# Inverse roots of variances and squared norms as powers on GpSimd

## The reference, cut to what matters

```python
# in each of the 6 layers
qkv = x @ Wqkv                        # 16 heads of 64
q = l2norm(q) * qs                    # t / max(norm(t), 1e-12), per head and token
k = l2norm(k) * ksc
...                                   # rotary, softmax(q k^T * 8) in windows of 32, values
mu = x.mean(-1, keepdims=True)
var = ((x - mu) ** 2).mean(-1, keepdims=True)
xn = (x - mu) / jnp.sqrt(var + 1e-05) * g + bln
...                                   # a * gelu(gate) @ W2 + b2
```

## Time and profile before

| | us |
|---|---|
| Median of three runs | 3716.87 (3713.0 to 3719.67) |
| The profiled execution, its time | 3724.61 |
| Its span | 3722.6 |
| PE busy | 3402.5 (91%) |
| DVE busy | 3223.6 (87%) |
| ACT busy | 2227.8 (60%) |
| POOL busy | 2052.1 (55%) |

### The profile page before, as it was taken

The page is one execution under the profiler, slowest core; times in us unless marked ns, Lnnn a source line. Parts: engine busy times, 40 slices in busy tenths (PEclk is TensorE's granted clock), DMA queues, the critical chain, the costliest instruction groups (busy, mean ns, idle before and its releaser), DMA issues.

```text
span 3722.6 us, 144192 instructions
## 1 busy us (share of the span) xinstructions
PE 3402.5 (91%) x62248; PEld 1871.9 (50%) x62248; DVE 3223.6 (87%) x5344; ACT 2227.8 (60%) x3808; POOL 2052.1 (55%) x1787
## 2 busy tenths in 40 slices
PE   6899999999999999985676799999999999999996
PEld 2455555555555555542333355555555555555553
DVE  5899999999999999874776799999999999999984
ACT  3566576665666666652453466666766667666663
POOL 3666566555666656642433565665656656565552
PEclk8999999999999999996877999999999999999998
DMA  4232332232332322200001332232232332332320
GB/s 126 68 79 70 75 81 73 72 81 70 80 77 70 85 70 72 73 17 12 0 0 54 78 76 73 70 87 69 73 85 67 78 83 67 77 82 66 77 49 24
DMA packets 200483, 250.08 MB, mean 67 GB/s; under 512 B 52012, under 2 KB 95656, under 8 KB 199848
## 3 DMA queue, kind: packets, MB, share of 16 engines
q1 hardware_dynamic: 199848, 240.86, 25.9%
HBM read 36.18 MB, written 3.15 MB: 11 GB/s over the span
## 4 chain that ended last, share of the span: by engine, by line
PE 30%; DVE 12%; issue 4%; ACT 3%; POOL 1%; DMA 1%; SPq 0%; POOLq 0%; DVEq 0%; ACTq 0%
PE general L566 4%; PE attp L580 4%; PE general L628 3%; PE scores L598 3%; PE sums L608 2%; PE general L636 2%; PE general L645 2%; PE general L638 1%; PE proj_k L554 1%; DVE k_ring L1232 1%; DVE sines L752 1%; DVE q_ring L758 1%; DVE probs_t L845 1%; PE proj_q L554 1%; PE proj_q L556 1%
## 5 line engine op out<-in xcount | busy, mean ns | idle before, releaser
L1107 POOL TENSOR_TENSOR k_ring<-k_ring,partner 128x512 f32<-128x512 f32 x384 | 499.0, 1299 | 362.1 <-DMA partner<-sines 359.9
L1116 POOL TENSOR_TENSOR probs<-probs,q_scale 128x512 f32<-128x512 f32 x384 | 401.8, 1046 | 396.8 <-DVE probs L828 396.8
L1122 POOL TENSOR_TENSOR probs<-probs,row_sum 128x512 f32<-128x512 f32 x384 | 407.8, 1062 | 358.3 <-DVE row_sum L839 358.2
L1107 POOL TENSOR_TENSOR q_ring<-q_ring,partner 128x512 f32<-128x512 f32 x384 | 491.2, 1279 | 50.4 <-DMA partner<-sines 50.4
L954 ACT ACTIVATE squares<-proj_q 128x512 f32<-128x512 f32 x384 | 229.0, 596 | 402.4 <-PE proj_q L556 401.0
L580 PEld LDWEIGHTS attp<-probs_t,v_buf 32*64 32x64 f32 x24576 | 393.0, 133 | 147.4 <-issue 141.8
L566 PE MATMUL general<-att,wo 128*128 128x512 f32 x768 | 376.2, 624 | 74.0 <-ACT att L1013 74.0
L580 PE MATMUL attp<-probs_t,v_buf 32*64 32x64 f32 (+1 forms) x24576 | 435.5, 218 | 5.1 <-ACT att L1013 5.1
L752 DVE SCALAR_TENSOR_TENSOR sines<-proj_q,vec,consts 128x512 f32<-128x512 f32 x384 | 278.7, 726 | 170.1 <-ACT squares L954 149.7
L628 PE MATMUL general<-wv,xs 128*32 128x256 f32 x6144 | 413.2, 387 | 3.1 <-DVE rstd L727 1.7
L598 PE MATMUL scores<-k_ring,q_ring 64*32 64x64 f32 (+1 forms) x24576 | 405.0, 215 | 0.0
(11 more groups left out here) (149 smaller groups left out, 6835.5 us busy)
## 6 DMA issues: line engine op xcount, KB each, us to landing
partner<-sines SPq DMA_DIRECT2D x3072, 64.0 KB
wqk_raw<-in_wqkv SPq DMA_DIRECT2D x80, 128.0 KB
wv<-in_wqkv SPq DMA_DIRECT2D x12, 512.0 KB, 4.4
wo<-in_wo SPq DMA_DIRECT2D x12, 512.0 KB, 4.7
w<-in_w SPq DMA_DIRECT2D x12, 341.0 KB, 3.3
base_dram<-x SPq DMA_DIRECT2D x8, 256.0 KB, 2.7
att<-in_wqkv SPq DMA_DIRECT2D x4, 512.0 KB, 5.8
q_ring<-base_dram SPq DMA_DIRECT2D x8, 256.0 KB, 3.1
```

The source lines that it names most:

```text
L1107: e.tensor_tensor(y, y, partner[:, which, :], ALU.add).then_inc(S[f"rotated_{side}"], 1)
L1116: e.tensor_tensor(y, y, spread_keys(scale), ALU.mult).then_inc(S["q_norms_off"], 1)
L1122: e.tensor_tensor(y, y, spread_keys(row_sum[:, b, :]), ALU.mult).then_inc(S["probs_done"], 1)
```

## The change

The two inverse roots are each made one instruction on POOL: `tensor_tensor` with the operation `pow` and an exponent of -0.5, which is held in a new tile `half` of one column and read as 512.

* `pool_scale` first raises `rstd` (variance plus epsilon) to -0.5 over the whole 128 x 512 tile, in place. DVE's turns L731 and L738, its reciprocal L733 and ACT's root L935 go. In the order of POOL the new instruction stands where `pool_scale` stood, after the rotations of step 0.
* A new `pool_norms` raises `inv_norm` to -0.5 over 128 x 512, in place. It stands at the head of POOL's step 0, before `pool_scores`. DVE's turn L787 and reciprocal L789 go from step 0, and ACT's root in place, L988, from step 1.
* DVE still turns once, at the head of step 1, but in the other direction: `inv_norm` to `norm_t`, which only the scale of q now reads. ACT's four small instructions stay, as copies with the factor 8 in place of roots, and wait for that turn. `inv_hi` waits for the power alone.
* ACT thus runs no root at all any more.

```diff
         def dve_var(...):
             e.tensor_scalar(rstd[:, :], general_of(("var", key))[:, :], EPS, None, ALU.add).then_inc(S["ln_var_kept"], 1)
-            w.wait_ge(S["ln_var_kept"], i + 1)
-            w.wait_ge(S["ln_rstd_turned"], i)
-            w.wait_ge(S["k_norms_turned"], turned["norms"])
-            e.transpose(var_t.rearrange("p w k -> p (w k)"), rstd[:, :]).then_inc(S["ln_var_turned"], 1)
-            w.wait_ge(S["ln_var_turned"], i + 1)
-            e.reciprocal(var_t[:, :, 0:1], var_t[:, :, 0:1]).then_inc(S["ln_inv"], 1)
-        def dve_root(e, w, key):
-            i = LN_ORDER[key]
-            w.wait_ge(S["ln_rstd"], i + 1)
-            e.transpose(rstd[:, :], var_t[:, :, 0:1].broadcast_to([P, ITEM_WINS, WIN])).then_inc(S["ln_rstd_turned"], 1)
-            turned["roots"] = i + 1
...
         def dve_norms(e, w, k, n):
             m = k * ITEMS + n
             w.wait_ge(S["squares_summed"], (m + 1) * (PAIRS // 2))
             w.wait_ge(S["inv_lo"], m)
+            w.wait_ge(S["sums_turned"], m)
             e.tensor_scalar(inv_norm[:, :], sums[:, :], 1e-24, None, ALU.max).then_inc(S["sums_kept"], 1)
-            w.wait_ge(S["sums_kept"], m + 1)
-            w.wait_ge(S["k_norms_turned"], m)
-            w.wait_ge(S["ln_rstd_turned"], turned["roots"])
-            e.transpose(norm_t.rearrange("p w h -> p (w h)"), inv_norm[:, :]).then_inc(S["sums_turned"], 1)
-            w.wait_ge(S["sums_turned"], m + 1)
-            e.reciprocal(norm_t[:, :, 0:NORM_ROWS], norm_t[:, :, 0:NORM_ROWS]).then_inc(S["sums_inverted"], 1)

         def dve_norms_back(e, w, k, n):
             m = k * ITEMS + n
-            w.wait_ge(S["k_root"], m + 1)
-            e.transpose(inv_norm[:, :], norm_t.rearrange("p w h -> p (w h)")).then_inc(S["k_norms_turned"], 1)
-            turned["norms"] = m + 1
+            w.wait_ge(S["sums_inverted"], m + 1)
+            w.wait_ge(S["q_scaled"], m * Q_SCALES)
+            e.transpose(norm_t.rearrange("p w h -> p (w h)"), inv_norm[:, :]).then_inc(S["sums_turned"], 1)
...
-        def act_root(e, w, key):
-            w.wait_ge(S["ln_inv"], LN_ORDER[key] + 1)
-            e.activation(var_t[:, :, 0:1], var_t[:, :, 0:1], ACT.Sqrt).then_inc(S["ln_rstd"], 1)
...
         def act_norms(e, w, k, n):
-            w.wait_ge(S["sums_inverted"], m + 1)
+            w.wait_ge(S["sums_turned"], m + 1)
...
-                e.activation(q_scale8[WIN * q:WIN * q + WIN, n % 2, :, :], src, ACT.Sqrt, scale=QK_SCALE * QK_SCALE)\
+                e.activation(q_scale8[WIN * q:WIN * q + WIN, n % 2, :, :], src, ACT.Copy, scale=QK_SCALE)\
                     .then_inc(S["q_scaled"], 1)
-            w.wait_ge(S["q_scaled"], (m + 1) * 4)
-            e.activation(norm_t[:, :, 0:NORM_ROWS], norm_t[:, :, 0:NORM_ROWS], ACT.Sqrt).then_inc(S["k_root"], 1)
...
         def pool_scale(e, w, key, dst):
-            w.wait_ge(S["ln_rstd_turned"], LN_ORDER[key] + 1)
+            i = LN_ORDER[key]
+            w.wait_ge(S["ln_var_kept"], i + 1)
+            w.wait_ge(S["half_set"], 1)
+            e.tensor_tensor(rstd[:, :], rstd[:, :], half[:, 0:1].broadcast_to([P, COLS]), ALU.pow).then_inc(S["ln_rstd"], 1)
+            w.wait_ge(S["ln_rstd"], i + 1)
             e.tensor_tensor(dst, centered[:, :], rstd[:, :], ALU.mult).then_inc(S["ln_scaled"], 1)
...
+        def pool_norms(e, w, k, n):
+            m = k * ITEMS + n
+            w.wait_ge(S["sums_kept"], m + 1)
+            w.wait_ge(S["half_set"], 1)
+            e.tensor_tensor(inv_norm[:, :], inv_norm[:, :], half[:, 0:1].broadcast_to([P, COLS]), ALU.pow).then_inc(S["sums_inverted"], 1)
...
             for st in PLAN:
+                if st.norms is not None:
+                    pool_norms(e, w, k, st.norms)
                 if st.exps:
                     pool_scores(e, w, k, *st.exps)
```

More of the change, by code:

```diff
@@ L44 @@
 NORM_ROWS = 2 * GROUPS
+Q_SCALES = 4
 C_IDENT, C_CENTER, C_MEAN, C_SUMSEL = 0, P, 2 * P, 2 * P + 1
@@ L257 @@
 SEMS = """consts_loaded recast_loaded vec_loaded bf16_consts ones_set shift_zeroed x_loaded x_turned x_kept
-ln_centered ln_kept ln_squared ln_var ln_var_kept ln_var_turned ln_inv ln_rstd ln_rstd_turned ln_scaled ln_affine
+ln_centered ln_kept ln_squared ln_var ln_var_kept ln_rstd half_set ln_scaled ln_affine
 shifted raw_loaded first_loaded wqk_hi wqk_lo wv0_loaded wv1_loaded wo_loaded w1_loaded w2_loaded
 xs_hi xs_lo proj_q proj_k squared_q squared_k cos_q cos_k sin_q sin_k moved_q moved_k rotated_q rotated_k
-squares_summed sums_kept sums_turned sums_inverted q_scaled k_root k_norms_turned inv_hi inv_lo
+squares_summed sums_kept sums_turned sums_inverted q_scaled inv_hi inv_lo
 v_projected v_kept norm_spread k_inv_kept scored k_norms_off row_max max_off q_norms_off exponent row_sum row_inv
@@ L307, in macaron_kernel @@
         partner = sb("partner", [P, 2, COLS])
+        half = sb("half", [P, 1])
         inv_norm = sb("inv_norm", [P, COLS])
@@ L319, in macaron_kernel @@
         rstd = sb("rstd", [P, COLS])
-        var_t = norm_t
         hidden = sb("hidden", [P, len(HIDDEN_CUTS), COLS])
@@ L680, in tensor_stack @@
                     pe_out(e, w, k, *st.out_first)
-        turned = {"norms": 0, "roots": 0}
         def vector_program(e):
@@ L727, in dve_var @@
             e.tensor_scalar(rstd[:, :], general_of(("var", key))[:, :], EPS, None, ALU.add).then_inc(S["ln_var_kept"], 1)
-            w.wait_ge(S["ln_var_kept"], i + 1)
-            w.wait_ge(S["ln_rstd_turned"], i)
-            w.wait_ge(S["k_norms_turned"], turned["norms"])
-            e.transpose(var_t.rearrange("p w k -> p (w k)"), rstd[:, :]).then_inc(S["ln_var_turned"], 1)
-            w.wait_ge(S["ln_var_turned"], i + 1)
-            e.reciprocal(var_t[:, :, 0:1], var_t[:, :, 0:1]).then_inc(S["ln_inv"], 1)
-        def dve_root(e, w, key):
-            i = LN_ORDER[key]
-            w.wait_ge(S["ln_rstd"], i + 1)
-            e.transpose(rstd[:, :], var_t[:, :, 0:1].broadcast_to([P, ITEM_WINS, WIN])).then_inc(S["ln_rstd_turned"], 1)
-            turned["roots"] = i + 1
         def dve_enter(e, w, k, c, stage):
-            (dve_center, dve_var, dve_root)[stage](e, w, ("enter", k, c))
+            if stage < 2:
+                (dve_center, dve_var)[stage](e, w, ("enter", k, c))
         def dve_rotate(e, w, k, n, p, which):
@@ L872, in vector_stack @@
                     dve_norms_back(e, w, k, st.norms_back)
-                if st.root is not None:
-                    dve_root(e, w, ("ffn", k, st.root))
                 if st.norms is not None:
@@ L945, in act_enter @@
                 return
-            act_root(e, w, ("enter", k, c))
             w.wait_ge(S["ln_scaled"], LN_ORDER["enter", k, c] + 1)
@@ L1029, in scalar_stack @@
                     act_norms(e, w, k, st.norms_back)
-                if st.root is not None:
-                    act_root(e, w, ("ffn", k, st.root))
                 if st.now:
@@ L1070, in gpsimd_program @@
             w = Waits(e)
+            e.memset(half[:, :], -0.5).then_inc(S["half_set"], 1)
             e.memset(k_inv[:, 0:WIN], 1.0).then_inc(S["ones_set"], 1)
@@ L1253, in do @@
                 elif i in (2, 5):
-                    dve_root(e, w, ("scan", c, i // 3))
+                    return
                 elif i == 7:
@@ L1324, in do @@
                 elif i in (2, 5):
-                    act_root(e, w, ("scan", c, i // 3))
+                    return
                 elif i == 7:
@@ L1368, in do @@
                     pool_scale(e, w, key, centered[:, :])
+                    w.wait_ge(S["m_loaded"], 48)
                     pool_affine(e, w, key, m_xn, mcol(M_G), mcol(M_B))
```

2 lines of the change are left out of this document (1 added, 1 removed).

## The result

The changed kernel takes 12791.49 us (median of 4 runs, 12788.12 to 12794.49) against 3718.27 us for the kernel before beside it (4 runs, 3713.0 to 3720.07): 3.441 times as long, with an interval from 3.435 to 3.4469. Its profiled execution took 12788.12 us. The forecast was 4790 us in a range from 3690 to 6560. The direction was right, and both powers stand on the item's path as forecast; what was wrong is one term, the duration of the power.

The account below looks back on a forecast made before the run. PE was taken as the bound except around step 0, where DVE and ACT are. 48 items at 16.7 + 3 us plus 125 us for other layer norms add 1071 to 3716.9: about 4790 us, range 3690 to 6560.

Parts of the forecast that it names:

- The duration d: Time of one 128 x 512 power on POOL, taken as 10 us, with bounds of 1.05 and 25.
- The page on POOL: Skill page's estimates for a power of 24 dependent steps: 41 us, or 3.4 well scheduled; totals about 8360 or 3950 us.
- The sum: 48 items at 16.7 + 3 us, plus 125 us for other layer norms: 1071 us added at d = 10.
- 2d - 3.3: Lengthening of one item, in us, for d above 2.2, from both powers in POOL's queue; 16.7 at d = 10.
- d - 2.2: Cost of each of 16 layer norms outside the items: pays d, gains a 2.2 us chain; 7.8 us each.
- the threshold: d = 2.2 us, above which an item grows by 2d - 3.3, below it by d - 1.1.
- The hand-over at step 1: DVE stands still 2.0 us while ACT's four copies wait for its turn and ACT's squares of q stand behind them.
- What PE sees: PE's spreading of step 2 needs `inv_lo`, behind DVE's turning; 0.4 us of slack, so an item grows 16.7 us.
- The clock: PE runs at a lower granted clock after two idle waits: 0 to 5 us an item, 3 taken at d = 10.
- a long program: Rival, chance 0.22: POOL's power takes d above 20 us; 6004 us at d = 20, 6564 at d = 25.
- The cheap power: Rival, chance 0.10: POOL's power costs a multiply, d = 1.05; an item is 0.05 us shorter, total 3697 us.
- DVE shut out during the power: DVE's L828, with two SBUF inputs, held through the second power: 3.4 us an item, 163 us in all; left out.

Follow-up runs that it names:

- both_mult: The changed kernel with each power replaced by a multiplication by a constant, so no inverse roots are computed; 3757.36 us, 1.0096 times the kernel before.
- pow_shapes: The kernel before with a row of power instructions of several shapes put on POOL at its start; 4518.58 us (one run).

## Why the prediction was right in its structure and wrong in its size

**The duration d: wrong, and the whole of the miss.** The step that failed is "I take d = 10 and keep 1.05 and 25". It is 82. Both ends came from rows that had nothing to do with a power. The middle went from a reciprocal on DVE to a power on POOL, through the ratio 1.54 of two multiplications; that ratio was measured on multiplications, which take 2 ns a column on POOL, and the power takes 159. The upper end was a count of 64 steps at 0.39 us, called a guess, and it cut off the range. At that same 0.39 us an 82 us power is some 210 steps; a count of steps had no row behind it.

**The page on POOL.** The Trainium skill, "GPSIMD Engine Reference", section 7, on dependent steps of 4 cycles, gave an estimate of 41 us with 24 steps and a sum of 8360 us. The measured duration is twice that estimate, and the run doesn't show how many steps the power has; of the two estimates from the page the slow one was the nearer.

**The sum: right.** With d = 82.2 the sum 2d - 3.3 gives 161.1 us more for an item; the mean items differ by 161.9. The 16 normalisations outside the items, at d - 2.2, give 80 us each. What 48 items of 161.9 leave of the 9064 us between the two spans is 1292, or 81 each. With its own 5 us for the clock the sum would have been 12,970 us, 2% of the excess too high. "Moves the time by 112 us for each us" was 112 far above the threshold and 101 just above it.

**The hand-over at step 1: right** (2.0 forecast, 2.01 in the timeline above), and as the sum had it, hidden under the second wait: it decides nothing in the changed kernel. In `both_mult` it is the larger of the two waits that grew on DVE, 90 us of 154.

**The way to PE: another than forecast, at the same length.** DVE's turning L827 waits for POOL twice an item (82.14 and 78.84), as forecast. But "What PE sees" led both powers to PE through that turning and `inv_lo`. PE's first wait runs through ACT: its exponential L992 waits 83.27 us for POOL's L1098, and the attention copy, for which PE waits, stands behind it. PE's second wait ends at POOL's affine L1069 (77.5 us of idle at 4282.48, 3703 us in all), with `inv_lo` following at 4287.03 in the same seam. Both ways hang on the same two powers, so at d = 82 the sum is the same. That a wrong path gave the right sum is luck; at d = 1.05 it didn't. No root is left on ACT, and its busy time falls by 296 us (2227.8 to 1931.7).

**The clock: right in kind, too high in size.** 5 us an item were set for a long program. The mean item is 161.9 - 161.1 = 0.8 us longer than the sum without a clock term. PE's matmuls did become 4.3 us longer, so most of that lay under waits, or the sum without the clock is a little too high; the runs don't tell which. In the five microseconds after the second power the granted clock is 0.50 (1.2 GHz), in the next 0.68, and then 1.00:

```profile
4280.20:4285.20 5.00, 2.71 (x3) 1.00 (x4) 0.83 (x2) 1.81 (x3) 4.90 (x5) 0.50 0.00 0
4285.20:4290.20 5.00, 5.00 (x15) 1.24 (x13) 4.21 (x7) 2.82 (x6) 2.63 (x3) 0.68 0.22 54
4290.20:4295.20 5.00, 4.84 (x150) 3.40 (x151) 4.94 (x10) 4.28 (x5) 3.57 (x3) 1.00 0.32 78
```

**The cheap power: wrong by 60 us.** At d = 1.05 the sum promised 3697, and `both_mult` took 3757. The step that failed is "an item is 0.05 us shorter": the mean item there takes 67.22 us, 0.9 more, 43 us in all. The sum followed DVE alone. It left out that ACT's exponential waits for the same POOL instructions and stands ahead of the attention copy on which PE waits. That this path, and not DVE's, makes the 0.9 us is argued from the waits above and not tested by itself. The rest of the span, with the 16 normalisations outside, is 8 us shorter, where the sum had 18.

**DVE shut out during the power: left out, rightly,** but for a reason that the prediction didn't have; see the last section.

## What to carry to other kernels

A function that no row of the trace shows should be run by itself before it is put into a kernel, and until then its upper bound is open: a ratio between engines that comes from multiplications says nothing of a function. If such an instruction's time goes by columns and not by partitions, as here, turn the tile so that only distinct values are raised: for the variances 16 columns cost 3 us, and 512 columns, which hold each value many times over, cost 82. The norms would need 128 columns, 20.7 us by `pow_shapes`; no run tried that. And the narrow power still lost to DVE's reciprocal and ACT's root, by its whole length wherever nothing else was in flight to hide it. And work moved to an engine with "room on average" counts by what stands behind it in that engine's order, here two instructions on which DVE, ACT and PE wait.

## What the runs showed of the hardware

**A power on POOL** costs 159 ns for each column of f32 on 0.35 us of start, the same for 1, 8, 32 and 128 partitions and for the exponents and inputs tried (128 x 512: 81.9 us; a multiplication of the same shape 1.04).

**POOL keeps DVE out only at the start of a power.** DVE's and POOL's timelines of the changed kernel, two stretches:

```profile
1001.22 0.38 DVE L751 TENSOR_TENSOR wqk_lo<-wqk_raw,wqk_hi 128x256 fp32r<-128x256 f32 x1
...
7432.97 0.96 DVE L810 TENSOR_TENSOR probs<-probs,row_max 128x512 f32<-128x512 f32 x1
```

```profile
997.49 82.39 POOL L1063 TENSOR_TENSOR rstd<-rstd,half 128x512 f32<-128x512 f32 x1
...
7432.34 81.93 POOL L1063 TENSOR_TENSOR rstd<-rstd,half 128x512 f32<-128x512 f32 x1
```

Both DVE instructions have two SBUF inputs. L751 starts 3.7 us into a power that has 79 us to go, and takes 0.38 us, as much as with POOL idle; ten such starts in this trace are alike. L810 starts 0.6 us into a power and takes 0.96 us, where 0.68 is its time with POOL idle; it ends 1.6 us after the power's start, with 80 us of the power to go. Two others that start 1.9 us into a power take 0.68. In the earlier trace rows POOL's instructions were 1.2 to 1.3 us long, and L828 didn't end before the one beside it had. The Trainium skill, "Advanced Engine Details and Errata", section Miscellaneous Facts, states that POOL and DVE share a read and a write interface and conflict when DVE has two SBUF inputs. The trace agrees for the first microsecond or so of a power and not for the rest, so a power is no block of 82 us for DVE; what DVE waits for is POOL's results. The power pays for the meeting too: the 47 of the variances that begin while L810 is running take 82.4 us, and the one above, with L810 behind its start, 81.9. That is most of the difference between the means 82.3 and 81.9 at the top; the multiplications in the same two places differ likewise, 1.41 against 1.04 us.
